# Second projection of a graph-attention layer in two column passes, with the attention terms of its rows as two extra columns, W2's halves spread over other groups, and the output bias on another engine

## The reference, cut to what matters

```python
# N = 1250 nodes, D = 768, 20000 edges + self loops twice, H = 4 heads of C = 512
def gat(x, W, a_src, a_dst, bias, concat):
    h = (x @ W).reshape(N, H, C)
    al_s, al_d = einsum('nhc,hc->nh', h, a_src), einsum('nhc,hc->nh', h, a_dst)
    e = leaky_relu(al_s[src] + al_d[dst], 0.2)
    ex = exp(e - segment_max(e, dst)[dst])
    out = segment_sum(h[src] * ex / segment_sum(ex, dst)[dst], dst)
    return out (heads concatenated, or their mean) + bias
h = elu(gat(layernorm(x), W1, ..., concat=True))      # 1250 x 2048
x = x + gat(h, W2, ..., H=1, C=768, concat=False)     # second layer: W2 is 2048 x 768
x = x + moe_ffn(layernorm(x))                         # router, shared expert, 8 experts, top 2
```

## Time and profile before

| | |
|---|---|
| three runs | 1328.58, 1319.58, 1327.04 us (median 1327.04) |
| the profiled execution | 1322.85 us |
| its span | 1321.1 us |
| mean granted TensorE clock | 0.967 of full speed |
| PE busy | 1207.5 us (91%) |
| VectorE busy | 873.4 us (66%) |
| ScalarE busy | 609.4 us (46%) |
| GpSimd busy | 161.9 us (12%) |

### The profile page before, as it was taken

How to read it: one execution, slowest core, us unless ns; L and a number is a source line. 1 busy time by engine, 2 the same in 40 slices (tenths; PEclk the granted TensorE clock), 3 DMA queues, 4 the chain that set the end, 5 groups by cost and what they waited for, 6 DMA issues and landing times.

```text
span 1321.1 us, 18384 instructions
## 1 busy us (share of the span) xinstructions
PE 1207.5 (91%) x7111; PEld 802.9 (61%) x7111; DVE 873.4 (66%) x1766; ACT 609.4 (46%) x1108; POOL 161.9 (12%) x144
## 2 busy tenths in 40 slices
PE   4887778888999799999999999999998799999996
PEld 3665443444555455545788888888556566666664
DVE  7889879988997899898543652444786323333330
ACT  5679356476546554876403650102311144444441
POOL 1000000000000000000000004000103734333322
PEclk9998999988999899999999999998999899999999
DMA  8344530462145323412753206213201587677532
GB/s 185 125 143 145 147 97 20 122 164 81 44 129 158 89 57 102 124 36 78 267 158 103 78 15 178 70 41 102 72 1 47 160 225 180 171 177 181 162 63 32
DMA packets 70210, 149.66 MB, mean 113 GB/s; under 512 B 10629, under 2 KB 34693, under 8 KB 69498
## 3 DMA queue, kind: packets, MB, share of 16 engines
q1 hardware_dynamic: 63467, 131.23, 33.2%
q0 software_dynamic: 6656, 17.26, 6.8%
HBM read 115.88 MB, written 34.59 MB: 114 GB/s over the span
## 4 chain that ended last, share of the span: by engine, by line
PE 58%; DVE 21%; issue 6%; ACT 6%; DMA 4%; SPq 2%; POOL 2%; POOLq 0%; DVEq 0%; ACTq 0%
PE PS L1775 47%; PE PS L1918 6%; DVE sb L1421 3%; DVE sb L1400 3%; DVE sb L1436 2%; DVE sb L1429 2%; SPq L541 2%; DVE sb L1288 1%; DVE sb L1470 1%; DVE sb L1371 1%; DVE sb L1481 1%; DMA sb<-aa_d 1%; POOL sb L850 1%; DMA sb<-in_L_ffn_w_dram 1%; DVE sb L1317 1%
## 5 line engine op out<-in xcount | busy, mean ns | idle before, releaser
L1775 PE MATMUL PS<-sb,sb 128*125 128x384 f16 (+8 forms) x4404 | 780.5, 337 | 45.3 <-DVE sb L1293 27.0
L1775 PEld LDWEIGHTS PS<-sb,sb 128*125 128x125 f16 (+3 forms) x4404 | 541.0, 128 | 269.0 <-issue 55.6
L1918 PE MATMUL PS<-sb,sb 125*128 125x375 f16 (+1 forms) x1440 | 263.1, 343 | 0.0
L1918 PEld LDWEIGHTS PS<-sb,sb 125*128 125x128 f16 x1440 | 140.5, 98 | 119.7 <-issue 9.5
L1619 DVE SCALAR_TENSOR_TENSOR sb<-sb,sb 128x2304 f16<-128x2304 f32 x27 | 68.8, 2557 | 84.5 <-ACT sb L1143 84.5
L1016 ACT ACTIVATE sb<-sb 125x375 f32<-125x375 f32 (+1 forms) x150 | 81.4, 543 | 83.6 <-DVE sb L1421 83.2
L830 POOL TENSOR_TENSOR sb<-sb,sb 125x768 f32<-125x768 f32 x10 | 18.0, 1838 | 803.2 <-DMA sb<-in_x_dram 803.2
L1421 DVE SCALAR_TENSOR_TENSOR sb<-sb,sb,sb 125x375 f32<-125x375 f32 (+1 forms) x150 | 95.6, 638 | 5.6 <-ACT sb L1010 5.4
L1010 ACT ACTIVATE sb<-sb,sb 125x375 f32<-125x375 f32 (+1 forms) x150 | 93.7, 628 | 0.7 <-DMA sb<-aa_d 0.7
L1429 DVE SCALAR_TENSOR_TENSOR sb<-sb,sb 125x375 f32<-125x375 f32 (+1 forms) x150 | 87.7, 585 | 1.2 <-ACT sb L1016 1.1
L1436 DVE TENSOR_TENSOR sb<-sb,sb 125x375 f16<-125x375 f32 (+1 forms) x150 | 87.9, 586 | 0.1
(11 more groups left out here) (188 smaller groups left out, 1062.0 us busy)
## 6 DMA issues: line engine op xcount, KB each, us to landing
sb<-in_L_ffn_w_dram SPq DMA_DIRECT2D x24, 1152.0 KB, 5.7
sb<-in_L_gnn_W_dram SPq DMA_DIRECT2D x32, 384.0 KB, 4.6
sb<-xt_d SPq DMA_DIRECT2D x30, 375.0 KB, 4.9
sb<-mask_d SPq DMA_DIRECT2D x20, 546.9 KB
sb<-h_d SPq DMA_DIRECT2D x10, 1000.0 KB, 5.4
h_d<-sb SPq DMA_DIRECT2D x16, 375.0 KB, 4.8
sb<-aa_d SPq DMA_DIRECT2D x5, 1093.8 KB
h_d<-sb SPq DMA_DIRECT2D x8, 500.0 KB, 5.0
```

Source lines behind the costliest of these rows:

```text
L1775: ins = M(out_, lhs(a), rhs(b), start=first and a + b == 0, stop=last and a == 1)
L1918: ins = M(PS[:, t, 0:n], hb[:, i, pa, 128 * c:128 * c + 128], P[:, i, pb, lo:lo + n], start=i == 0 and pa + pb == 0, stop=i == NT - 1 and ...
```

## The change

Five things are changed together:

1. v2 no longer has matmuls of its own. It becomes two columns in front of W2's 768: `W2S[ch]` is 772 wide, and VectorE copies v2's halves in (`V.tensor_copy`, one for each chunk) just before the low half. `al2`, `al2_columns`, `SEL` and the copy of the rows are gone.
2. The second projection runs as 20 units in two passes: units 0 to 9 make 322 columns (v2 and 320 of W2's) of tiles 0 to 9, units 10 to 19 the other 448 columns, in the order 9, 2, 3, ..., 8, 0, 1. Eight places hold loaded tiles, five of them in `P`'s memory, so that only tiles 0 and 1 are loaded twice. A unit uses one bank; six take turns.
3. `chain_row`, `chain_max`, `chain_shift` and `P`'s steps for the second layer move to the second pass, since the terms are complete only behind the first. `p_hi` waits for the units that still read tiles in `P`'s memory.
4. `W2_STEPS` begins one group earlier (the sixth group, g = 5) and ends earlier; `load_ht(0)` moves behind three W2 loads.
5. x plus the output bias (`x_bias`) is added on VectorE in the second attention's loop, no longer on GpSimd.

```diff
-        W2_STEPS = [0, 0, 0, 0, 0, 0, 1, 1, 1, 2, 2, 2, 2, 2, 2]
+        W2_STEPS = [0, 0, 0, 0, 0, 1, 1, 2, 2, 2, 2, 2, 2, 1, 0]
-        P2_STEPS = [0, 0, 0, 0, 6, 6, 6, 6, 6, 2]
+        P2_STEPS = [0] * (NT + 4) + [5, 5, 5, 5, 6, 0, 6]
+        DA = 320
+        HALF_B = [9, 2, 3, 4, 5, 6, 7, 8, 0, 1]
+        HT_SLOT = [0, 1, 3, 4, 5, 6, 7, 2, 1, 0, 2, 1]
+        def bank2(u):
+            return (6, 7, 0, 1, 2, 3)[u % 6]
+        def w2_part(q):
+            return slice(0, DA + 2) if q == 0 else slice(DA + 2, D + 2)
...
@@ SP, second projection
-            load_ht(0)
             for ch in range(8, 11):
                 load_w2(ch)
+            load_ht(0)
+            load_w2(11)
             store_h1(NB * H - 2)
-            for ch in range(11, 14):
+            for ch in range(12, NCH):
                 load_w2(ch)
             load_ht(1)
...
+            load_ht(2)
             store_h1(NB * H - 1)
...
+            for v in range(3, NT):
+                load_ht(v)
...
             chain_row(H)
...
             chain_shift(H)
...
+            for v in range(NT, NT + 2):
+                load_ht(v)
+            sp.wait_ge(s_pj2, 2 * NT)
@@ GpSimd
-            pool.wait_ge(s_bias, 48)
-            for j in range(NT):
-                pool.wait_ge(s_xr[j], 32)
-                nc.gpsimd.tensor_tensor(X2[:, j, :], X2[:, j, :], B2R[:, :], ALU.add).then_inc(s_xb, 1)
@@ ScalarE, p_hi
                 act.wait_ge(s_p4, q + 1)
+                if h == H and b == 0:
+                    act.wait_ge(s_pj2, NT + 2 + min(4, (4 * N * i + 4 * N - 1) // 8000))
@@ VectorE
             def w2_lo(ch):
                 dve.wait_ge(s_w2h, ch + 1)
-                V.scalar_tensor_tensor(W2S[ch][:, 1, :], W2G[ch % 3][:, :], SW, W2S[ch][:, 0, :], ALU.mult,
+                if ch in (0, V2_FIRST):
+                    dve.wait_ge(s_vs, 1 if ch == 0 else 2)
+                V.tensor_copy(W2S[ch][:, :, 0:2], V2S[:, ch, :, :])
+                V.scalar_tensor_tensor(W2S[ch][:, 1, 2:D + 2], W2G[ch % 3][:, :], SW, W2S[ch][:, 0, 2:D + 2], ALU.mult,
                                        ALU.subtract).then_inc(s_w2l, 1)
...
+            for u in range(NT):
+                h2_lo(u)
+            chain_row(H)
+            for u in range(NT, NT + 3):
+                h2_lo(u)
+                for j in range((0, 4, 8)[u - NT], (4, 8, NT)[u - NT]):
+                    chain_max(H, j)
             chain_shift(H)
...
+            def x_bias(j):
+                if j == 0:
+                    dve.wait_ge(s_bias, 48)
+                dve.wait_ge(s_xr[j], 32)
+                V.tensor_tensor(X2[:, j, :], X2[:, j, :], B2R[:, :], ALU.add).then_inc(s_xb, 1)
+
+            x_bias(0)
             for j in range(NT):
...
                                 ALU.mult).then_inc(s_xn2, 1)
+                if j + 1 < NT:
+                    x_bias(j + 1)
@@ TensorE
                     b, c = g // (CH + 1), g % (CH + 1) - 1
-                    if c == CH - 1 and NB * h + b:
-                        al2(NB * h + b - 1)
...
+            for u in range(2 * NT):
+                q = u // NT
+                ht, arrived, value = ht_use(u)
                 pe.wait_ge(arrived, value)
+                if 2 <= u < 6:
+                    pe.wait_ge(s_y1, CH * NB * H - 5 + u)
+                if u >= 6:
+                    pe.wait_ge(s_h2l, h2_made(u - 6))
...
                 for ch in range(NCH):
+                    if u == 0:
                         pe.wait_ge(s_w2l, ch + 1)
+                    if u == NT and ch == 4:
+                        chain_row(H)
+                    if u == NT + 3 and ch == 8:
+                        chain_shift(H)
+                    ins = mm3(PS[0:T, b, 0:part.stop - part.start], lambda a: ht[:, a, ch, :],
+                              lambda r: W2S[ch][:, r, part], ch == 0, ch == NCH - 1)
                 ins.then_inc(s_pj2, 1)
```

More of the change, by code:

```diff
@@ L213, in build @@
     V2F = small([128, NCH, 2], F32)
-    V2S = small([128, NCH, 20], F16)
-    SEL = small([12, NB, 2], F32)
+    V2S = small([128, NCH, 2, 2], F16)
     AL = small([T, 2, H + 1, NT], F32)
@@ L428, in step, with half_tile, ht_use @@
             return NT * (NB * h + b) + i
[L430 to L432 removed]
+        HALF_A = list(range(NT))
+        HALF_B = [9, 2, 3, 4, 5, 6, 7, 8, 0, 1]
+        HT_SLOT = [0, 1, 3, 4, 5, 6, 7, 2, 1, 0, 2, 1]
+        def half_tile(u):
+            return (HALF_A + HALF_B)[u]
+        def ht_use(u):
+            v = half_tile(u) if u < NT or half_tile(u) >= 2 else NT + half_tile(u)
+            return HT[HT_SLOT[v]], s_ht[v % 4], 16 * (v // 4 + 1)
         def v2_in(ch):
@@ L707, in _, with load_ht @@
                         load_w2(ch)
-            def load_ht(j):
-                place, arrived, value = ht_use(j)
-                if j == 0:
+            def load_ht(v):
+                if v == 0:
                     sp.wait_ge(s_h1s[(NB * H - 3) % 2], 32 * ((NB * H - 3) // 2 + 1))
@@ L820, in _ @@
             link(nc.gpsimd.memset(big[:, :], -NEG))
-            link(nc.gpsimd.memset(SEL[:, :, :], 0.0))
-            for part in range(2):
-                link(nc.gpsimd.affine_select(out=SEL[:, :, :], in_=SEL[:, :, :], compare_op=ALU.not_equal, fill=1.0,
-                                             base=-2 * part, pattern=[[-4, NB], [-1, 2]], channel_multiplier=1))
-            pool.wait_ge(s_bias, 48)
-            for j in range(NT):
-                pool.wait_ge(s_xr[j], 32)
-                nc.gpsimd.tensor_tensor(X2[:, j, :], X2[:, j, :], B2R[:, :], ALU.add).then_inc(s_xb, 1)
             pool.wait_ge(s_at2, NT)
@@ L1115, in _ @@
             A(WRS[:, :, 0, :], WRG[:, :, :], ACT.Copy, scale=SW).then_inc(s_wh, 1)
-            for j in range(NT):
-                p_steps(H, P2_STEPS[j])
-                h2_hi(j)
+            for u in range(2 * NT):
+                p_steps(H, P2_STEPS[u])
+                h2_hi(u)
+            p_steps(H, P2_STEPS[2 * NT])
             assert p_made[H] == NT * NB + 2
@@ L1575, in _ @@
                                    ).then_inc(s_wl, 1)
-            h2_lo(0)
-            for j in range(NT):
-                chain_max(H, j)
+            for u in range(NT):
[5 more added lines that the diff above has]
+                    chain_max(H, j)
             chain_shift(H)
-            h2_lo(1)
             chain_shift_rows(H)
-            for j in range(2, NT):
-                p_steps(H, P2_STEPS[j])
-                h2_lo(j)
+            h2_lo(NT + 3)
+            for u in range(NT + 4, 2 * NT):
+                p_steps(H, P2_STEPS[u])
+                h2_lo(u)
+            p_steps(H, P2_STEPS[2 * NT])
             def x2t_lo(i):
@@ L1923, in att @@
                 ins.then_inc(s_att, 1)
-            def al2(k):
-                h, b = divmod(k, NB)
-                n, nj = DB[b][1], len(TB[b])
-                pe.wait_ge(s_y6, CH * (k + 1))
-                if k in (0, NB * (H - 1)):
-                    pe.wait_ge(s_vs, 1 if k == 0 else 2)
-                for c in range(CH):
-                    for part in range(2):
-                        ins = M(PS[0:12, 4, 0:n], V2S[:, CH * h + c, 8 - 4 * b:20 - 4 * b],
-                                H1O[k % 2][:, part, 0:nj, c, :], start=k + c + part == 0,
-                                stop=k == NB * H - 1 and c == CH - 1 and part == 1)
-                ins.then_inc(s_a2, 1)
-            def al2_columns():
-                pe.wait_ge(s_const, 16)
-                pe.wait_ge(s_a2r, 1)
-                for b in range(NB):
-                    for j in TB[b]:
-                        lo = T * (j - TB[b].start)
-                        ins = M(PS[0:T, 5, 2 * j:2 * j + 2], A2W[:, lo:lo + T], SEL[:, b, :], start=True, stop=True)
-                ins.then_inc(s_a2c, 1)
             for h in range(H):
@@ L1999, in _ @@
                 b = 4 + 2 * (j % 2)
-                for i in range(NT):
+                order = HALF_B if j == 0 else HALF_A
+                for i in order:
                     if j == 0:
-                        pe.wait_ge(s_h2l, 3 * (i + 1))
+                        pe.wait_ge(s_h2l, h2_made(NT + HALF_B.index(i)))
                     for b_ in range(NB):
@@ L2007, in _ @@
                         ins = mm3(PS[0:T, b + q, 0:n], lambda a: P[:, i, a, T * j:T * j + T],
-                                  lambda r: H2[i][:, r, lo:lo + n], i == 0, i == NT - 1)
+                                  lambda r: H2[i][:, r, lo:lo + n], i == order[0], i == order[-1])
                 ins.then_inc(s_at2, 1)
```

149 lines of the change are left out of this document (58 added, 91 removed).

## The result

The changed kernel took 1331.78 us (median of 15 runs, 1326.64 to 1335.80), the kernel before, on the same chip, 1326.69 (15 runs). The ratio is 1.0047 with a 95% interval of 1.0034 to 1.0060: 6.2 us slower, 4.5 to 8.0 (the two medians alone lie 5.1 apart). That is inside the 1% that the prediction called no change, and larger than what the runs leave open. A second series of the same kernel gave 1331.25 and 1.0050 [1.0028, 1.0072].

What follows compares the result with a forecast made beforehand. VectorE and a broadcast's round trip were taken to set the heads' pace, TensorE the second projection and second attention. +1.9 us for the passes' end and +1.5 for the clock made +3.4: forecast 1328 us, range 1322 to 1336.

Steps and rivals of the forecast that it cites:

- The v2 matmuls of the heads: First layer's attention: of some 16 us freed on TensorE only 1.0 comes back; the wait before head 2's projection grows.
- The first rival: All of TensorE's freed time comes back, 16 us in the heads and 5.5 in the projection: 1302 to 1306; chance 0.05.
- W2's halves: VectorE in head 3: earlier halves and 16 copies of v2 (1.6 us) add 2.8 us up to the last low half.
- The first unit waits: Second projection's start: TensorE stands some 6 us for W2's last low half at 654.5; the unit ends at 654.9.
- The rest of both passes: Second projection after its first unit: 150.3 us, ending at 805.2; the end moves by +1.9 us at most.
- The clock: TensorE at half speed behind the first unit's new wait: 1.5 us lost, of 0 to 2.6.
- The projection's own v2 work: Second projection: v2's matmuls and the slowed ones behind them go, together 5.5 us credited.
- Loads: Tiles of h for pass 1, 1 MB each 6.6 us: the places suffice, costed at 0.
- `P` of the second layer and x plus bias: Second pass and second attention: `P` hides with 23 us to spare; VectorE's ten additions fit its waits: 0 on the path.
- The signs: What the profile should show: head 2's projection near 441, `P` 2 to 3 us later, second pass between 712 and 718.
- W2 not being what unit 0 waits for: Rival, second projection's start: last low half comes by 648 to 651, the projection's 5.5 us show: 1319 to 1324; chance 0.2.
- `P` late: Rival: second attention's first tile waits for `P`'s block 0, 10 to 20 us: 1338 to 1348; chance 0.09.

Runs made afterwards that it cites:

- e13: The changed kernel run again unaltered, in a later batch: 1331.25 us, ratio 1.0050 to the kernel before.
- e4: The kernel before with one matmul in place of eight in v2's first eleven passes over h (heads only): 1321.91 us, ratio 0.9983.
- e12: The kernel before with v2's TensorE work cut in heads and projection: one matmul of eight per pass, one small one of twenty: 1319.09 us, ratio 0.9958.
- e5: The kernel before with v2's work cut only in the second projection (one matmul of eight, one small one of twenty): 1321.95 us, ratio 0.9977.
- e3: The changed kernel with x plus output bias back on GpSimd before the second attention: 1331.63 us, ratio 1.0044 to the kernel before.
- e6: The kernel before with the changed kernel's numbers for W2's halves, begun one group earlier: 1327.12 us, ratio 1.0024.
- e2: The changed kernel with W2's halves made by the old numbers, from the seventh group on: 1328.73 us, ratio 1.0025 to the kernel before.
- e1: The changed kernel with its first two projection units interleaved from chunk 14, tile 1's h loaded four W2 loads earlier: 1325.86 us, ratio 1.0004 to the kernel before.
- e11: The changed kernel with its first two units interleaved from chunk 12, tile 1's h loaded behind W2's chunk 13: 1322.45 us, ratio 0.9982 to the kernel before.
- e10: The changed kernel with the old numbers for W2's halves and its first two units interleaved from chunk 12: 1326.05 us, ratio 1.0010 to the kernel before.

## Why the prediction came out right, point by point

The time: 1328 forecast, 1331.8 measured; no change at 1%, slower by 0.5%. The sum was +3.4 us on the profile, which showed +3.9 of span and +4.1 of time; the ratios of two series say +6. The size is short by some 2.5 us. That the profile agrees within 0.5 us is partly luck: in it head 2's projection began 1.65 us earlier than before and took 1.25 us less, and neither is shown to belong to the change (e13, the same kernel, began at 444.15).

Measured from the end of head 2's projection, the last low half came 2.9 us later than before (3.3 in e13); the forecast has 2.5 there, 2.8 less the 0.3 that it credits to head 2. From the last low half to the end of the passes it took 3.5 us more than before (3.2 in e13), where the sum has 1.5 for the clock and nothing besides. Together that is 6.4 and 6.5 us. So the mechanism was right, and three terms were too small: the clock most of all, by 1.4 us (1.1 in e13), the passes by 0.7 and the last low half by 0.4 to 0.8.

- **The v2 matmuls of the heads: right.** 1.0 us taken, 0.3 to 16 as bounds; e4 gives 2.3 (-0.9 to 5.3), and the wait grew by nearly what was freed. A', which begins behind head 1 and for which 0.3 was credited, is 0.3 to 0.6 us shorter in e4 and e12 than in before and e5. The credit of the earlier heads is smaller than what two executions differ by there, so it is not shown. The first rival (1302 to 1306) fails by this.
- **W2's halves: right in size.** The sum had +2.8 us up to the last low half, 1.2 for the numbers and 1.6 for the copies; 2.9 and 3.3 were measured from the end of head 2's projection (5.4 in e3, with its long wait for a load). Two paths lead from the numbers to TensorE. One is the last low half, which the first unit waits for in the changed kernel. The other is `P`, 2.9 us later by A', which counts in full only where no wait for W2 follows, as in e6. The sum rightly took one of the two, not both. In e2, by the same measure from the end of head 2's projection, the last low half came 1.5 to 4.1 us sooner than in the three executions with the new numbers, which holds its 2.9 us. The 16 copies were priced at 1.6 us and cost 0.08 each on the path, 1.3. The Trainium skill (VectorE: DVE Perf Modes, on the TRN2 errata) has about 150 cycles for a small operation; the row's duration, 0.17 us, agrees, but VectorE started the next 0.08 us after the copy, so the estimate built on it was too high.
- **The first unit waits: right.** Two waits, 3.04 and 3.62 us, where some 6 were forecast; it ended 1.1 us behind the last low half by ScalarE's read, forecast 0.4, with its last matmuls at half clock. e1 and e11 show that this wait decides C.
- **The rest of both passes: right within a microsecond.** From the last low half on 150.7 us without the clock's part; 154.3, 154.0 and 153.6 measured with it, which leaves 151.4 in all three. Units take 6.56 and 9.1 us at full clock. (The end of the passes was forecast at 805.2, 1.7 us behind the 803.46 of before; the sum took 1.9.)
- **The clock: mis-sized.** 1.5 us taken of 0 to 2.6; 5.9 us at half clock in the profile, 2.9 lost, 5.2 us and 2.6 in e13, 4.4 and 2.2 in e3. This is the largest error of the sum. The upper bound was read too low as well: ahead of head 2 in the kernel before the clock was back at about 447.8, not 447, which makes 2.9 us lost. The Trainium skill (TensorE: Matmul & The Clock Gate, on the warmup) calls the size run-variable; these executions agree, with 2.2 to 2.9 us behind waits of the same place.
- **The projection's own v2 work: right on this profile.** 5.5 us credited; e5 shows 4.9 in C. Of that 1.6 are the clock, which in e4's execution didn't fall behind the same work.
- **Loads: right here, and thin.** No unit waited for its h in the changed kernel, but e10 shows what a late one costs (3.71 us). What it costs to hurry it, e1's rows suggest and don't show.
- **`P` of the second layer and x plus bias: right.** TensorE waited 0.32 us inside the second pass, at the shift's transpose, and not at all ahead of the attention; e3 shows no difference.
- **The signs.** Given as absolute times, they hold in the profile and not in every execution. Head 2's projection began at 440.32 (within 1.5 us of 441) but at 444.15 in e13; the second pass began near 715, between 712 and 718, but near 719 in e13, where the sign, taken by its words, says that the forecast is wrong. The last pieces of `P` came at 617.12 and 618.39 us in the profile, no later than before, and at 621.27 and 622.55 in e13; the delay of 2 to 3 us shows in A', which is 2.5 and 3.1 us longer.
- **The rivals.** W2 not being what unit 0 waits for: false, by the two waits. `P` late: false. Pass 1 not narrower: false, units are 6.6 us.

Where the gain went, on e12's scale: taking v2's matmuls away is worth 5.6 us and the whole change costs 6, so what came with it costs 12. Shown of that: about 6 by the short first unit with its wait and clock (e1; 8.8 with the better order, e11) and 3 by W2's earlier halves (e2). These may overlap, and up to three us stay open; the 0.3 us wait inside the second pass and the two added columns (0.4, worked out, not measured) are part of them.

What the runs don't settle: whether e11 with the old numbers would gain the 3 us of A as well. e10 was meant to show it and lost its gain to a late load. Open too is why ScalarE's wait for one and the same W2 load differs so much between executions with the same order of loads (1.74 us in e13, 4.31 in e3), though it moves C by up to 3 us.

## What to carry to other kernels

When a unit of work is made shorter, look at what its length was covering: here a 17 us first unit hid sixteen operands that were still being made, and a 6.6 us one stood for them and lost the clock too. Let two short units share such a wait by running the chunks that are ready of both, in an order that fits the order in which operands arrive, and see that the second unit's own input is there. Work on an engine that waits elsewhere comes back only where its own wait ends last: some 17 us of matmuls were worth 5.6.
